# A two-layer adaLN transformer block on one core: moving the output product and the fourth exponential in the issue order of the main attention

## What is computed

```
q, k: 16 heads of 128 + 64 columns, the 64 with rotary positions; v: 16 heads of 128
scores = q @ k.T * 192**-0.5           # 1024 x 1024 for each head
probs  = softmax(scores)
ctx    = probs @ v
x     += gate * (ctx of all heads side by side) @ o_w.T
```

## Time and profile before

| | us |
|---|---|
| median of 3 runs | 1260.73 (1259.4 to 1261.2) |
| the profiled execution's own time | 1260.88 |
| its span, first to last instruction | 1259.0 |
| TensorE busy in the span | 1177.3 |
| VectorE busy | 890.4 |
| ScalarE busy | 654.0 |
| GpSimd busy | 532.2 |

### The profile page before, as it was taken

The page is one execution under the profiler, slowest core; times in us unless marked ns, Lnnn a source line. Parts: engine busy times, 40 slices in busy tenths (PEclk is TensorE's granted clock), DMA queues, the critical chain, the costliest instruction groups (busy, mean ns, idle before and its releaser), DMA issues.

```text
span 1259.0 us, 34623 instructions
## 1 busy us (share of the span) xinstructions
PE 1177.3 (94%) x14433; PEld 825.6 (66%) x14436; DVE 890.4 (71%) x1354; ACT 654.0 (52%) x1242; POOL 532.2 (42%) x531
## 2 busy tenths in 40 slices
PE   8999999999899999999998789999998998989997
PEld 5643434467677777777776577888653444778997
DVE  4689988448688887887788947456777753766555
ACT  3579988854344444444444334332455775345553
POOL 4256265325958777696764034452100000412221
PEclk8999999999899999999999889999999998899999
DMA  7870000011111111111111040110335100101111
GB/s 282 217 171 15 2 18 16 13 34 43 30 41 38 32 34 42 39 32 32 41 32 62 11 147 1 51 52 12 88 89 124 45 9 1 34 18 42 48 38 34
DMA packets 41699, 66.25 MB, mean 53 GB/s; under 512 B 8476, under 2 KB 27676, under 8 KB 40604
## 3 DMA queue, kind: packets, MB, share of 16 engines
q1 hardware_dynamic: 41544, 64.04, 18.8%
HBM read 45.60 MB, written 8.45 MB: 43 GB/s over the span
## 4 chain that ended last, share of the span: by engine, by line
PE 72%; DVE 14%; issue 4%; ACT 4%; POOL 3%; DMA 1%; SPq 1%; DVEq 0%; ACTq 0%; POOLq 0%
PE bank L1478 8%; PE bank L1938 7%; PE bank L2148 6%; PE bank L2149 6%; PE bank L2150 6%; PE bank L1569 5%; PE bank L1435 4%; PE bank L1834 4%; PE bank L1836 3%; PE bank L1835 3%; PE bank L1972 3%; PE bank L1298 3%; PE bank L1415 2%; DVE mpc L1377 2%; DVE nmq L1843 2%
## 5 line engine op out<-in xcount | busy, mean ns | idle before, releaser
L1456 ACT ACTIVATE Pb<-bank 128x512 f32<-128x512 f32 (+3 forms) x355 | 180.6, 574 | 29.7 <-PE bank L1435 8.9
L1843 DVE TENSOR_REDUCE nmq<-bank 128x1 f32<-128x1024 f32 x128 | 154.7, 1209 | 53.8 <-PE bank L1836 53.2
L1858 ACT ACTIVATE P<-bank,nmq 128x1024 f32<-128x1024 f32 x128 | 142.7, 1115 | 93.6 <-DVE nmq L1843 92.8
L1306 DVE TENSOR_REDUCE mp<-bank 128x2 f32<-128x1024 f32 x128 | 153.5, 1222 | 27.3 <-PE bank L1298 26.6
L1871 DVE STREAM_TRANSPOSE PT<-P 128x1024 f32<-128x1024 f32 x124 | 151.7, 1224 | 0.0
L1938 PE MATMUL bank<-PT,kv 32*64 32x128 f32 x7936 | 137.2, 276 | 11.7 <-issue 11.0
L1938 PEld LDWEIGHTS bank<-PT,kv 32*64 32x64 f32 x7936 | 118.7, 131 | 37.9 <-issue 37.8
L1377 DVE TENSOR_REDUCE mpc<-bank 128x2 f32<-128x1024 f32 (+2 forms) x96 | 88.3, 953 | 44.7 <-PE bank L1365 22.1
L1834 PE MATMUL bank<-qk1h,qk0h 128*128 128x512 f32 x256 | 111.5, 436 | 8.6 <-POOL qk0l L1676 4.0
L1478 PE MATMUL bank<-Pb,vx 128*17 128x256 f32 (+3 forms) x1222 | 107.2, 410 | 0.6 <-ACT OTa L1492 0.5
L1836 PE MATMUL bank<-qk1h,qk0l 128*128 128x512 f32 x256 | 101.9, 398 | 0.1
(11 more groups left out here) (354 smaller groups left out, 2881.2 us busy)
## 6 DMA issues: line engine op xcount, KB each, us to landing
t<-t SPq DMA_DIRECT2D x128, 64.0 KB, 2.4
wr<-wf SPq DMA_DIRECT2D x25, 256.0 KB, 2.7
wraw<-wf SPq DMA_DIRECT2D x8, 768.0 KB, 4.5
scratch<-stgr SPq DMA_DIRECT2D x4, 1024.0 KB, 4.0
Rs<-shares SPq DMA_DIRECT2D x64, 64.0 KB, 2.8
scratch<-stg SPq DMA_DIRECT2D x8, 384.0 KB, 2.6
qst<-scratch SPq DMA_DIRECT2D x9, 256.0 KB, 8.3
owT<-owT SPq DMA_DIRECT2D x1, 2048.0 KB, 11.6
```

Of the source, the lines that this page charges most:

```text
L1306: e.tensor_reduce(mp[:, w % 3, :, j, kh], wide[slot][:], AX, ALU.max).then_inc(ring_ok, 1)
L1456: e.activation(PBR[l][i % len(PBR[l])][:, 0:c], bank[b][:, 0:c], ACT.Exp, scale=0.25).then_inc(exp_ok[0], 1)
L1843: e.tensor_reduce(nmq[:, n % 8:n % 8 + 1], scores(u, i), AX, ALU.max, negate=True).then_inc(mp_ok, 1)
L1858: e.activation(probabilities(u, i)[:], scores(u, i), ACT.Exp, bias=nmq[:, n % 8:n % 8 + 1], accum_out=sums[:, u % 2, i:i + 1]).then_inc(ex ...
```

## The change

Two steps move in the list, and nothing else does. The pair `project u-2`, `add u-2` goes from behind `score u 0` to behind `score u 1`, in all units but the last. `expo u 3` goes from the end of the unit to in front of `lift u-1`. On TensorE the output product so stands behind the second score tile, and in units with two `prep` the first of them stands ahead of it. On VectorE the `add` moves behind `rec u-1`, `vturn u-1 3` and the maxima of tile 1. On ScalarE the fourth exponential comes ahead of the two copies of `lift`.

```diff
     for u in range(1, 32):
         order.append(("score", u, 0))
-        output(u - 2)
+        if u == 31:
+            output(u - 2)
         prep(4 * u, "prep")
         order.extend([("rec", u - 1), ("spread", u - 1), ("vturn", u - 1, 3), ("expo", u, 0)])
         prep(4 * u, "pcopy")
         order.extend(BESIDE_LAST.get((u, 0), ()))
         order.append(("score", u, 1))
+        if u < 31:
+            output(u - 2)
         prep(4 * u + 1, "prep")
         prep(4 * u + 1, "pcopy")
         order.extend([("vturn", u, 0), ("expo", u, 1)])
         order.extend(BESIDE_LAST.get((u, 1), ()))
         order.extend([("score", u, 2), ("pv", u - 1, 0), ("vturn", u, 1), ("expo", u, 2)])
-        order.extend([("score", u, 3), ("pv", u - 1, 1), ("lift", u - 1), ("vturn", u, 2), ("ot", u - 1), ("expo", u, 3)])
+        order.extend([("score", u, 3), ("pv", u - 1, 1), ("expo", u, 3), ("lift", u - 1), ("vturn", u, 2), ("ot", u - 1)])
```

## The result

The changed kernel takes **1269.06 us** (median of 5 runs, 1268.46 to 1276.87), the kernel before 1260.73 (median of 5 beside it, 1257.87 to 1261.2). The ratio is 1.0089, 95% interval 1.0056 to 1.0121: slower by 0.9%. It is the ratio of the means (1271.20 and 1260.02), which stands above that of the medians, 1.0066. The forecast was 1270.1. The profiled execution of the changed kernel took 1273.14 us, 4.1 over its median, with a span of 1271.3.

What follows compares the result with a forecast made beforehand. The prediction took TensorE as the bound, with VectorE close behind. Its terms, 3.0 + 3.1 + 0.6 + 1.2 + 1.5 = +9.4 us, on 1260.73 gave 1270.1 us, range 1262 to 1278.

Steps and rivals of the forecast that it cites:

- (a): Output product waits for `OTm` in no one-prep unit; in two-prep units the first `prep` waits instead, about 0.9 us each.
- (b): In one-prep units the product of values waits for the `add`, about 0.5 us each, some 7 to 10 us in all.
- (c): The weighing's wait for `lift` grows from 25.6 to 35 to 40 us; `lift` follows the fourth exponential by 0.12 us.
- (d): Clean units take 12.9 to 13.1 us with one prep, about 14.2 us with two.
- (e): Unit 30, without preps, takes about 12.75 us, where it took 11.53 us.
- Unit 31: Weighing must wait for the fourth exponential and `lift`, +1.0 us, and the unit starts 0.45 us later: +1.5 us.
- the twelve units with two preps: Units 7 to 28 with two preps: later `lift` lengthens seven by about 0.43 us, five unchanged: +3.0 us.
- the twelve with one: Units 5 to 26 with one prep: longer loop through the late `add` and later `lift`, +3.1 us.
- unit 29: No prep, but extra work on VectorE: +0.6 us.
- 4 us either way: Allowance for the issue gaps, matmul waits at the products of values, said to move with the phase of the DMAs.
- simply hidden: Rival: first `prep` and product of values find inputs ready, 12.6 us saved, 1248.1 us; chance 0.07 together with a partial form.
- GpSimd holds L1894: Rival: the tiny product takes 1 us in most one-prep units, +16.4 us in all, 1277 us; chance 0.13.

Runs made afterwards that it cites:

- the swap alone: Kernel before with only the fourth exponential moved ahead of `lift`; output product and `add` stay: 1268.37 us, ratio 1.0060.
- the move alone: Changed kernel without the earlier fourth exponential: only output product and `add` go behind score tile 1, against the kernel before: 1259.75 us, ratio 1.0011.
- the best kernel: Changed kernel with `add` early and first `prep` behind the output product, units 29 to 31 in the old order: 1255.59 us, ratio 0.9962.

## Why the prediction was right

Forecast +9.4 us, measured +8.3 in the medians and +11.2 in the means (ratio 1.0089). Its five signs, one by one.

(a) *The output product stops waiting; `prep` takes over.* Right: 13 waits at the matmul for 6.8 us and at the weight load for 12.4 us, 0.95 each. The swap alone shows the 0.45 us in it at the output product itself, and with the first `prep` put behind, the units with two preps fall from 14.2 or 14.5 us to between 13.3 and 13.9. So it was the wait of this `prep` that kept them.

(b) *The product of values waits for the `add`.* Right. Of the 10.3 us in units 5 to 30 some 6.9 stand in the twelve units with one prep, about 0.6 us each where the forecast had 0.5, and just under the 7 to 10 us that it gave in all; the other 3.4 stand in units 28 to 30, which this sign left out. Shown by the early `add`, with which no product waits for it. The profile calls this wait "issue" in all rows of the changed kernel that I read.

(c) *`lift` behind the fourth exponential.* Right: 0.11 us after it in unit 14, 34.0 us of waits for it at L1960, just under the 35 to 40 that I gave.

(d) *Clean units.* Undisturbed units with two preps take 14.17 (unit 23, below: first maximum to first maximum) to 14.23 us where u % 4 is 3, which is the 14.21 of the forecast, and 14.46 where it is 0, which is 0.45 over their 14.00 before.

```profile
597.88 1.22 DVE L1846 TENSOR_REDUCE nmq<-bank 128x1 f32<-128x1024 f32 x1
...
612.05 1.22 DVE L1846 TENSOR_REDUCE nmq<-bank 128x1 f32<-128x1024 f32 x1
```

With one prep the loop closes as described, but I made it 0.2 us too long. Units 14, 17, 21 and 13 take 12.57, 12.77, 12.92 and 13.29 us with L1897 at 0.16, 0.38, 0.51 and 0.89: always 12.4 us and L1897 on top. I had 12.95 with 0.34 us in it, so 12.6 on top. The other parts are right to 0.01 us (3.71, 2.49 and 1.70 in unit 14); the one that is off is "maximum to product of values 5.05", which is 4.67 with L1897 at 0.16, so 4.85 at 0.34. The 0.2 us were in the stretch of VectorE in unit 9 that I took for unbroken work (the `add`, then the output product in front of it on TensorE):

```profile
396.97 0.69 DVE L1985 TENSOR_TENSOR x<-x,bank 128x512 f32<-128x512 f32 x1
```

The output product ends at 396.93 (395.80 + 1.13), the maximum in front of the `add` at 396.88 (395.66 + 1.22), and the `add` starts 1.31 us after that maximum starts; in 25 of the 27 units from 5 to 31 of the kernel before it is 1.30 or 1.31 us. In the changed kernel, where the output product has long been done, it is 1.10 to 1.14, by the timeline of unit 14 1.11 (474.33 - 473.22). So the stretch held 0.20 us of waiting for TensorE, which the profile doesn't mark, and which the change took away: 2.4 us too much over twelve units.

(e) *Unit 30, 12.75 us*: 12.55, the same 0.2. *Unit 31*: +1.0 up to the weighing, as forecast, and by the chain that it named, maximum, exponential, `lift`, weighing. All five traces with the swap in unit 31 have this 1.0 us, and none of the others. The 0.45 us that the forecast added for a later start of the unit came to 0.13 (score tile to first maximum 1.93 us where it was 1.80), since the product in front of it was stretched by 0.3 us.

```profile
728.38 1.19 DVE L1846 TENSOR_REDUCE nmq<-bank 128x1 f32<-128x1024 f32 x1
...
729.60 1.11 ACT L1861 ACTIVATE P<-bank,nmq 128x1024 f32<-128x1024 f32 x1 [1.12 <-DVE nmq L1846]
...
730.83 0.78 ACT L1952 ACTIVATE other<-bank 64x256 f32<-64x256 f32 x2
...
731.71 0.43 DVE L1960 TENSOR_TENSOR bank<-bank,other 128x256 f32<-128x256 f32 x1 [0.94 <-ACT other L1952]
```

Term by term, in the profiled executions: the twelve units with two preps +2.2 (forecast +3.0); the twelve with one +7.3 (+3.1); unit 29 +3.1 (+0.6); unit 30 +1.0 (+1.2); unit 31 +1.0 (+1.5). The largest miss is in units 6 and 9, whose first product of values was stretched to 3.87 and 3.62 us where it had taken 2.03 and 2.02: they account for 4.4 of the 7.3 us. That is the "4 us either way" of the issue gaps, spent on the slow side; that they move with the phase of the DMAs, as the forecast had it, no run shows. The first products of units 6 and 9 have gaps of 1.4 to 2.2 us in all six traces with both parts of the change, and in none of the eight others, so they are likely to belong to the change and not to chance; what causes them stays open.

The step that failed is the term for **unit 29**, "no prep, but extra work on VectorE: +0.6". The extra work now lies ahead of the `add`:

```profile
690.04 1.23 DVE L2276 TENSOR_TENSOR wl<-wraw,wh 128x1024 fp32r<-128x1024 f32 x1 [0.33 <-ACT wh L2271]
691.18 1.22 DVE L1846 TENSOR_REDUCE nmq<-bank 128x1 f32<-128x1024 f32 x1
692.32 0.68 DVE L1988 TENSOR_TENSOR x<-x,bank 128x512 f32<-128x512 f32 x1
...
693.10 2.96 PE L1941 MATMUL bank<-PT,kv 32*64 32x128 f32 x128 [2.31 <-issue]
```

```profile
693.00:698.00 5.00, 4.90 (x134) 4.17 (x134) 3.41 (x3) 1.85 (x4) 0.00 (x0) 0.66 0.10 29
```

TensorE waits 2.31 us, and then the granted clock, 1.00 in the 5 us before, has a mean of 0.66 (the windows view again): a good part of the 5 us at the lower level, 1.2 GHz. The 128 matmuls take 2.96 us instead of 2.08. The swap alone makes unit 29 longer by 0.8 us (13.62 where it was 12.86) and the move alone, with a wait of 2.20 us for the `add` but the clock at 1.00, by 1.05 us (13.91): 1.8 us together, three times the 0.6 of the forecast. The remaining 1.3 us are left for the lower clock. The wait was there to be computed from the trace of before, in which the split of 1.22 us stands in the same unit; the clock wasn't in the forecast at all.

That the total came within 1.1 us is in part luck. The loop that was 0.2 us too long gave 2.4 us too much, unit 29 gave 2.5 too little, and the gaps of units 6 and 9, of which the forecast knew nothing, are set off elsewhere: unit 12 has lost a gap and takes 2.0 us less, and 3.6 us came back behind the stage.

Of the rivals, "simply hidden" fell with the waits at `prep` and `add`. "GpSimd holds L1894" came true in a small part at most: L1897 has a mean of 0.56 us in the twelve units with one prep up to 27, where it had 0.51 (the 0.46 of the forecast counts units 29 and 30 in), so 0.6 us in all and not 7, with single rows of 0.89 to 1.15 us (units 13, 22, 26). That the whole came to 8.3 us while the traced execution lost 13.6 us in units 5 to 30 has two reasons: this execution is 4.1 us over the median, and 3.6 us came back behind the stage, where no instruction of the change stands. Between two traces of the kernel before that part differs by 0.3 us, but over all fourteen traces it lies between 525.6 and 532.2, so I don't read it as an effect.

The two parts of the change: the swap alone +0.60% (0.25 to 0.96), the move alone +0.11% (-0.21 to +0.43), both +0.89% (0.56 to 1.21). The sum of the parts lies inside the interval of the whole. The `add` late by itself cost +0.60%, more than the move alone, of which it is a part; its trace puts most of it into units 28 to 30. The move alone took 41.9 us there, against 47.7, and its trace shows the difference: the gap in unit 28 is 1.65 us and not 3.87 (the unit takes 15.63 us and not 19.51), and in unit 29 the wait for the `add` is as long (2.20 us) but the clock stays at 1.00 (13.91 us and not 15.48). Why the gap and the clock differ is open.

## What to carry to other kernels

Before an instruction is moved to take away a wait, list all that waits for the same result, and all that is queued with it: here `prep` waited for the same `OTm` and stood in front, and the `add` moved behind two maxima, on an engine that had no slack in that stretch. The same idea won 0.4% (0.1 to 0.6) once all was moved that belonged to it (the `add` forward, the `prep` backward, the last three units left alone). When a wait goes, look whether it comes back under another name; a label such as "issue" may be a wait for another engine, which an end time 0.10 us before the start betrays.

## What the runs showed of the hardware

**Gaps come back.** With the waits at `OTm` and the `add` gone, the rest of the units fell by 10.8 us (341.2 to 330.4), but the stretched products rose by 8.9 (18.1 to 27.0). With `lift` first again the rest rose to 347.4, and the stretched products fell to 14.1. Inside a product of values all inputs are there from its start, so these are not waits for data. In unit 22 of the changed kernel both kinds of "issue" stand together:

```profile
586.41 1.83 PE L1941 MATMUL bank<-PT,kv 32*64 32x128 f32 x108 [1.22 <-issue]
...
590.32 0.65 PE L1941 MATMUL bank<-PT,kv 32*64 32x128 f32 x20 [2.08 <-issue]
```

The 1.22 us in front of the product are the wait for the `add`, which ended 0.10 us before it; the 2.08 us in front of its last 20 matmuls are a gap. In units 5 to 30 of all fourteen traces, whatever the order of the steps, every gap over 0.8 us inside a product stands at one of nine places: in the first product of units 6, 9, 12, 15, 19, 22, 25 with 32, 24, 17, 3, 32, 20 and 12 of the 128 matmuls left, and in the second product of units 5 and 28 with 1 and 4 left. Those of units 5, 15, 25 and 28 are in every trace (the one of unit 28 between 0.29 and 3.87 us long), unit 12 has it in eleven, unit 22 in ten, unit 19 in eight, units 6 and 9 in six. So the place is set as if by a count of instructions, and the length is not. Two executions of one kernel differ in it (unit 22 took 16.17 us in one trace of the kernel before and 12.55 in the other). A supply of instructions that can't keep up with short matmuls would fit: the engine catches up while it waits, and where it no longer waits, the gap is seen. No run shows the supply itself, and the extra transfers, which met none of the nine places, made no gap, so this is an argument and not a finding.

**Behind a short pause the clock can fall, and the length of the pause doesn't tell when.** After 3.87 us and after 2.3 us without matmuls the granted clock fell from 1.00 to means of 0.66 to 0.74 over the next 5 to 6 us. In unit 29 of the move alone TensorE waits 2.20 us in the same place, and the clock stays up (the product, then the windows view):

```profile
680.19 2.08 PE L1941 MATMUL bank<-PT,kv 32*64 32x128 f32 x128 [2.20 <-issue]
```

```profile
680.00:686.00 6.00, 5.81 (x263) 4.97 (x264) 5.61 (x6) 2.03 (x5) 0.00 (x0) 1.00 0.10 27
```

Behind the gap of unit 28 it fell after 1.66 us in the kernel with the early `add` (mean 0.57 over the next 4 us) and after 1.93 us in the best kernel (0.66 over 5 us); it stayed at 1.00 after 1.93 us in the swap alone and after 1.65 us in the kernel before. So a pause of 1.7 to 2.3 us goes either way here, and what decides isn't shown. A fall costs about 1.6 us, an estimate from unit 29 of the `add` late alone (15.48 us) and of the move alone (13.91), whose waits are 2.30 and 2.20 us but whose orders differ by more than the clock.

**One port, two engines.** The split of the experts' weights by VectorE took 1.22 us in the kernel before, where it started ahead of GpSimd's, and GpSimd's took 2.09; in the kernel with the early `add` and the late `prep` GpSimd came first, with 1.27, and VectorE's took 2.30. Both rows of each, the kernel before first:

```profile
679.71 1.22 DVE L2273 TENSOR_TENSOR wl<-wraw,wh 128x1024 fp32r<-128x1024 f32 x1
679.97 2.09 POOL L2294 TENSOR_TENSOR wl<-wraw,wh 128x512 fp32r<-128x512 f32 x1 [3.37 <-ACT wh L2288]
```

```profile
679.41 1.27 POOL L2301 TENSOR_TENSOR wl<-wraw,wh 128x512 fp32r<-128x512 f32 x1 [3.31 <-ACT wh L2295]
679.47 2.30 DVE L2280 TENSOR_TENSOR wl<-wraw,wh 128x1024 fp32r<-128x1024 f32 x1
```

That is the rule of the Trainium skill, SBUF — State Buffer, section "Who interferes with whom", cited ahead of the result: whoever comes second waits the other out. The traces agree in both orders.
